# A factor moved as a logarithm into the exponents of the decay matrices, and x copied unscaled by ScalarE

## The reference

```python
alpha = jnp.exp(dt * A)
gamma = lam * dt
beta = (1.0 - lam) * dt * alpha
def step(carry, inp):
    h, prevBx = carry
    x_t, B_t, C_t, a_t, g_t, b_t = inp
    Bx = jnp.einsum('bhp,bhn->bhpn', x_t, B_t)
    h = a_t[..., None, None] * h + g_t[..., None, None] * Bx + b_t[..., None, None] * prevBx
    y = jnp.einsum('bhpn,bhn->bhp', h, C_t)
    return ((h, Bx), y)
y = y + xh * D[None, None, :, None]
y = y * jax.nn.silu(z)
y = _rms(y, norm_w)
return y @ out_proj_w.T
```

## Time and profile before

| | before |
|---|---|
| median of 3 runs | 1303.15 us (1301.98 to 1310.49) |
| profiled execution | 1303.54 us, its span 1301.8 us |
| PE busy | 1149.1 us, 88% |
| DVE busy | 1193.7 us, 92% |
| ACT busy | 811.0 us, 62% |
| POOL busy | 739.4 us, 57% |
| granted TensorE clock, mean | 0.965 |

### The profile page before, as it was taken

The page is one execution under the profiler, slowest core; times in us unless marked ns, Lnnn a source line. Parts: engine busy times, 40 slices in busy tenths (PEclk is TensorE's granted clock), DMA queues, the critical chain, the costliest instruction groups (busy, mean ns, idle before and its releaser), DMA issues. The chain is left out here.

```text
span 1301.8 us, 30976 instructions
## 1 busy us (share of the span) xinstructions
PE 1149.1 (88%) x11530; PEld 837.3 (64%) x11530; DVE 1193.7 (92%) x1925; ACT 811.0 (62%) x1257; POOL 739.4 (57%) x592
## 2 busy tenths in 40 slices
PE   3787489998999999999999899989999899989996
PEld 3662266666666666666666667666667666666664
DVE  7988499998999899998999899989999899989994
ACT  4576166666666666667666666656666666666663
POOL 5000166665766566665766576656666576666664
PEclk9865699999999999999999999999999999999999
DMA  8533343234332153333333343234332333322330
GB/s 189 182 97 105 94 100 69 69 66 99 91 82 64 43 124 83 67 70 73 86 83 71 78 101 73 56 70 116 90 68 59 79 91 83 68 53 59 84 67 9
DMA packets 69664, 107.75 MB, mean 83 GB/s; under 512 B 14179, under 2 KB 32844, under 8 KB 69196
## 3 DMA queue, kind: packets, MB, share of 16 engines
q1 hardware_dynamic: 69516, 105.78, 34.8%
HBM read 24.73 MB, written 12.06 MB: 28 GB/s over the span
## 5 line engine op out<-in xcount | busy, mean ns | idle before, releaser
L1403 POOL TENSOR_TENSOR rot<-part 128x512 f32<-128x512 f32 x256 | 375.8, 1469 | 515.6 <-DVE part L1207 515.6
L1207 DVE SCALAR_TENSOR_TENSOR part<-bcs,k_prmT,k_trig 128x512 f32<-128x512 f32 x512 | 495.9, 1017 | 22.7 <-DMA bcs<-bc_t 12.1
L1340 ACT ACTIVATE E<-d 128x512 f32<-128x512 f32 x256 | 151.7, 592 | 186.4 <-PE d L1029 186.4
L1225 DVE TENSOR_TENSOR M<-s,E 128x512 f32<-128x512 f32 x256 | 163.2, 676 | 2.4 <-PE s L1047 1.8
L1047 PE MATMUL s<-rot 64*128 64x128 f32 x2048 | 149.7, 285 | 17.2 <-POOL rot L1403 17.1
L1047 PEld LDWEIGHTS s<-rot 64*128 64x128 f32 x2048 | 126.9, 188 | 55.1 <-issue 54.7
L1412 POOL TENSOR_TENSOR ce<-rot,eb 128x512 f32<-128x512 f32 x128 | 160.2, 1273 | 3.0 <-ACT eb L1373 3.0
L1456 POOL TENSOR_TENSOR sqa<-sqa,sq 128x512 f32<-128x512 f32 x112 | 142.5, 1273 | 14.5 <-ACT sq L1345 6.2
L1013 PE MATMUL r<-k_w_zx,xns 128*128 128x256 f32 x512 | 133.1, 382 | 12.1 <-DMA xns<-xn_t 12.1
L1136 PE MATMUL y<-M,xk 128*64 128x128 f32 x2048 | 140.1, 279 | 0.0
L1061 PEld LDWEIGHTS o<-k_w_o,yT 128*128 128x128 f32 x1024 | 132.5, 191 | 10.5 <-DVE yT L1298 5.0
(11 more groups left out here) (244 smaller groups left out, 1823.0 us busy)
## 6 DMA issues: line engine op xcount, KB each, us to landing
k_trig<-k_tri SPq DMA_DIRECT2D x512, 128.0 KB, 2.4
bcs<-bc_t SPq DMA_DIRECT2D x16, 256.0 KB, 3.9
bcs<-bc_t SPq DMA_DIRECT2D x32, 128.0 KB, 3.8
a_big<-in_L_attn_u SPq DMA_DIRECT2D x4, 512.0 KB, 6.1
xn_t<-a_xnT SPq DMA_DIRECT2D x1, 2048.0 KB, 14.7
tc_t<-a_tcT SPq DMA_DIRECT2D x1, 2048.0 KB, 16.8
bc_t<-a_tmp SPq DMA_DIRECT2D x1, 2048.0 KB, 7.7
gate_rows<-a_big SPq DMA_DIRECT2D x8, 256.0 KB, 2.0
```

The costliest lines, as they stand in the source:

```text
L1207: nc.vector.scalar_tensor_tensor(out=part[:, 2 * p + f, :], in0=bcs[:, (t + q // NQ) % 2, 2 * w + f, :], scalar=col, in1=trig[:, p, 1 - f, ...
L1225: nc.vector.tensor_tensor(M[:, h, :], Sp[h % 2][:], E[:, h % 2, :], ALU.mult).then_inc(m_ready, 1)
L1340: nc.scalar.activation(E[:, h % 2, :], Dp[:], ACT.Exp).then_inc(e_ready, 1)
L1403: nc.gpsimd.tensor_tensor(rot[:, q % 2, p, w, :], part[:, 2 * p, :], part[:, 2 * p + 1, :], ALU.add).then_inc(rot_ready, 1)
```

## The change

The state's input factor kk leaves x. For the decay matrices its logarithm is cut into three bf16 parts like the running sum and takes 12 more rows of K["pick"] (123 rows instead of 111), so that Exp gives exp(cum[t] - cum[s]) kk[s]. For the state, `dec` is multiplied by kk once in `prepare`. `xk` then holds plain x: ScalarE copies it, and DVE keeps only the product with `cc`, which waits for ScalarE's copy (`x_copied`) instead of PE's product.

```diff
@@ prepare: vector
-                for dst, head in PLACES:
-                    link(nc.vector.tensor_tensor(by4(K["kk"][:, a:b])[:, :, dst], by4(gam[:, a:b])[:, :, head],
-                                                 by4(ps[i][:])[:, :, head], ALU.add))
+                link(nc.vector.tensor_tensor(kk[:, a:b], gam[:, a:b], ps[i][:], ALU.add))
+                nc.vector.tensor_scalar(kk[:, a:b], kk[:, a:b], 0.0, TINY, ALU.max, ALU.add).then_inc(kk_done, 1)
@@ prepare: gpsimd (own_log, the mask of the new rows, is built before)
+            for i in range(2):
+                pool.wait_ge(log_cut, i + 1)
+                nc.gpsimd.tensor_tensor(s[2].rearrange("p (c h) -> p c h", h=H), s[2].rearrange("p (c h) -> p c h", h=H), cum3[:, :, H * i:H * i + H], ALU.subtract).then_inc(log_left, 1)
+            pool.wait_ge(dec_done, 1)
+            nc.gpsimd.tensor_tensor(K["dec"][:], K["dec"][:], kk[:], ALU.mult).then_inc(log_left, 1)
@@ prepare: tensor, in the loop of the gate
+                if t in (3, 4):
+                    pe.wait_ge(log_cut, 3)
+                    for g in (2 * t - 6, 2 * t - 5):
...
+                        for i in range(8):
+                            last = nc.tensor.transpose(ps_bf[g % 2][0:3 * H, i, :], cum3[:, 8 * g + i, :], K["ident_bf"][:])
+                        last.then_inc(logT_t, 1)
@@ prepare: scalar
+                if g == 2:
+                    act.wait_ge(kk_done, 2)
+                    nc.scalar.activation(s[2], kk[:], ACT.Ln).then_inc(log_left, 1)
...
+            def log_part(i):
+                act.wait_ge(log_left, i + 1)
+                act.wait_ge(cumT_t, 4)
+                nc.scalar.copy(cum3[:, :, H * i:H * i + H], s[2].rearrange("p (c h) -> p c h", h=H)).then_inc(log_cut, 1)
+
+            log_part(0)
             for t in range(NS):
                 if t + 2 < NS:
                     gate_input(t + 2)
+                if t in (1, 3):
+                    log_part((t + 1) // 2)
...
+                if t in (3, 4):
+                    act.wait_ge(cum_stored, 64)
+                    for g in (2 * t - 6, 2 * t - 5):
+                        act.wait_ge(logT_t, g + 1)
+                        nc.scalar.copy(cumT[:, 1024 * g:1024 * g + 1024],
+                                       ps_bf[g % 2][0:3 * H].rearrange("p c t -> p (c t)")).then_inc(logT_out, 1)
@@ prepare: sync
-            fill(cum[OWN_S:D_ROWS], own[OWN_S:D_ROWS, :], 8)
+            fill(cum[OWN_S:OWN_L], own[OWN_S:OWN_L, :], 8)
+            fill(cum[OWN_L:D_ROWS], own_log[OWN_L:D_ROWS, :], 8)
...
+                if t == 5:
+                    sp.wait_ge(logT_out, 4)
+                    for i in range(3):
+                        sp.dma_start(logs_d.rearrange("t c i h s -> i h (t c) s")[i],
+                                     cumT[H * i:H * i + H, :].rearrange("h (x s) -> h x s", s=P)).then_inc(logs_stored, 16)
@@ units: sync
+                sp.dma_start(K["pick"][OWN_L:D_ROWS, :], logs_d[t].rearrange("c i h s -> (c i) (h s)")).then_inc(cum_loaded, 16)
@@ units: vector, x_scaled
-                dve.wait_ge(x_ready, at(T2, t, 2 * q + i + 1))
+                dve.wait_ge(x_copied, at(T2, t, 2 * q + i + 1))
                 dve.wait_ge(y_ready, at(T2, t, 2 * q - 2))
-                for dst, f in ((xk, "kk"), (xc, "cc")):
-                    v = K[f][:, tt * (CS * H) + 2 * i * H:tt * (CS * H) + 2 * i * H + 2 * H].rearrange("p (c h) -> p c h", h=H)
...
@@ units: scalar
+            def x_copy(t, q, i):
+                act.wait_ge(x_ready, at(T2, t, 2 * q + i + 1))
+                act.wait_ge(y_ready, at(T2, t, 2 * q - 2))
+                nc.scalar.copy(xk[:, q % 2, 2 * i:2 * i + 2, :].rearrange("p c k -> p (c k)"), R[i][:]).then_inc(x_copied, 1)
...
                     decays(t, q, 2)
                     decays(t, q, 3)
+                    if live(t, q + 1):
+                        x_copy(t, q + 1, 0)
                     for p in range(2):
                         act.wait_ge(eb_ready, at(T2, t, 2 * q + p + 1))
                         act.wait_ge(ce_ready, at(T2, t, 2 * q - 1 + p))
                         nc.scalar.activation(eb[:, p, :], Dp[:], ACT.Exp).then_inc(ebs_ready, 1)
+                    if live(t, q + 1):
+                        x_copy(t, q + 1, 1)
```

More of the change, by code:

```diff
@@ L49 @@
 OWN_S = OWN_T + 3
-D_ROWS = OWN_S + 3 * CS
+OWN_L = OWN_S + 3 * CS
+D_ROWS = OWN_L + 3 * CS
 ODD_T = 123
@@ L299, in _ @@
                 link(nc.gpsimd.tensor_copy(tile[0:MASK_ROWS, 1:CS, :], bcast(tile[0:MASK_ROWS, 0:1, :], [MASK_ROWS, CS - 1, P])))
-            mine = own[OWN_T:D_ROWS, :].rearrange("r (c s) -> r c s", c=CS)
+            mine = own[OWN_T:OWN_L, :].rearrange("r (c s) -> r c s", c=CS)
             link(nc.gpsimd.memset(own[64:P, :], 0.0))
-            link(nc.gpsimd.memset(own[OWN_T:D_ROWS, :], -1.0))
+            link(nc.gpsimd.memset(own[OWN_T:OWN_L, :], -1.0))
             for base, mult in ((-3, 1), (5, -1)):
@@ L307, in _ @@
             link(nc.gpsimd.memset(own[OWN_T:OWN_S, :], 1.0))
+            mine = own_log[OWN_T:D_ROWS, :].rearrange("r (c s) -> r c s", c=CS)
+            link(nc.gpsimd.memset(own_log[OWN_T:D_ROWS, :], 1.0))
+            for base, mult in ((-3 - 3 * CS, 1), (5 + 3 * CS, -1)):
+                link(nc.gpsimd.affine_select(out=mine, in_=mine, compare_op=ALU.is_ge, fill=0.0, base=base,
+                                             pattern=[[-3 * mult, CS], [0, P]], channel_multiplier=mult))
             pool.sem_inc(masks, 1)
@@ L580, in _ @@
             link(nc.vector.scalar_tensor_tensor(out=s[1], in0=s[2], scalar=-1.0, in1=s[1], op0=ALU.add, op1=ALU.subtract))
-            link(nc.vector.scalar_tensor_tensor(out=s[0], in0=s[0], scalar=0.0, in1=K["kk"][:], op0=ALU.max, op1=ALU.add))
+            link(nc.vector.scalar_tensor_tensor(out=s[0], in0=s[0], scalar=0.0, in1=kk[:], op0=ALU.max, op1=ALU.add))
             dve.wait_ge(inv_done, 2)
@@ L809, in _, with units @@
                 nc.scalar.activation(fgate[:, t % 2, :], ps[2 + t % 2][:], ACT.Silu, scale=sc[:, 5:6]).then_inc(g_done, 1)
-def units(nc, K, u, scratch, cum_stored, out):
-    xn_d, tc_d, bc_d, cum_d, cumt_d, gate_d = scratch
+                if t in (3, 4):
[4 more added lines that the diff above has]
+                                       ps_bf[g % 2][0:3 * H].rearrange("p c t -> p (c t)")).then_inc(logT_out, 1)
+def units(nc, K, u, scratch, cum_stored, logs_stored, out):
+    xn_d, tc_d, bc_d, cum_d, cumt_d, gate_d, logs_d = scratch
     with ExitStack() as ctx:
@@ L870, in units @@
         xk_ready, bw_ready = sem("xk_ready"), sem("bw_ready")
+        x_copied = sem("x_copied")
         sz_ready, yt_ready, sq_ready = sem("sz_ready"), sem("yt_ready"), sem("sq_ready")
@@ L954, in _ @@
             sp.wait_ge(cum_stored, 64)
+            sp.wait_ge(logs_stored, 48)
             load_cum(0)
@@ L1318, in _ @@
             act.sem_inc(absd, 3)
-            for s in (e_ready, ebs_ready, sz_ready, sq_ready, acc_done):
+            for s in (e_ready, ebs_ready, x_copied, sz_ready, sq_ready, acc_done):
                 act.sem_inc(s, 1)
@@ L1360, in normalised @@
                 last.then_inc(acc_done, 1)
+            x_copy(0, 0, 0)
+            x_copy(0, 0, 1)
             decays(0, 0, 0)
@@ L1476, in program @@
         cum_stored = ctx.enter_context(nc.semaphore("cum_stored"))
-        prepare(nc, K, dram, scratch, cum_stored)
-        units(nc, K, dram[0], scratch, cum_stored, out)
+        logs_stored = ctx.enter_context(nc.semaphore("logs_stored"))
+        prepare(nc, K, dram, scratch, cum_stored, logs_stored)
+        units(nc, K, dram[0], scratch, cum_stored, logs_stored, out)
 NAMES = ["u", "in_proj_w", "dt_bias", "A_log", "D", "B_norm_w", "C_norm_w", "B_bias", "C_bias", "norm_w", "out_proj_w"]
```

40 lines of the change are left out of this document (25 added, 15 removed).

## The result

| | before | after |
|---|---|---|
| median | 1303.99 us (4 runs, 1301.98 to 1310.49) | 1327.59 us (4 runs, 1326.39 to 1329.10) |
| ratio to before | | 1.0173 (95% interval 1.0135 to 1.0210) |
| profiled execution | 1303.54 us | 1327.3 us, its span 1325.6 us |

The account below looks back on a forecast made before the run. It took the loop to be bound by a chain through PE's stretch from bw to x half 1 and DVE's half 1. Terms 15.8 + 6.4 + 0.5 - 0.6 = 22.1 on 1303.5 gave 1325 us, range 1308 to 1340.

Parts of the forecast that it names:

- The loop's chain: Per unit: bw, PE's stretch to x half 1, DVE's half 1, M2, M3, six rotations, two yT, bw; half 0 outside.
- Copy for product in half 1: In the chain, ScalarE's copy replaces DVE's product of 0.60 us, leaving the link as long: +0.01 to +0.03 us.
- The copy ahead of eb: ScalarE's half 0 copy makes the first eb 0.25 us later, delaying PE's second row exponents and x half 1 by 0.24.
- 63 x 0.25: The loop's loss: 63 units with a next unit, each 0.25 us longer, 15.8 us in all.
- Other consequences hide: In the loop, z, the table load and Silu, the 12 more rows and the extra transfer cost nothing.
- GpSimd in `prepare`: GpSimd's three 1024-column instructions beside DVE's `quantise` cost DVE 6.4 us, between nothing and 7.6.
- One more fill: SP issues one more fill ahead of the stores before the loop: +0.5 us (0 to 1).
- ScalarE's extra work hidden: In `prepare`, ScalarE's Ln, table load, casts and copies find gaps and cost nothing; uncovered, 1 to 2 us.
- Rival A: DVE itself is the loop, so two products fewer save 1.20 us per unit: 1234 us; chance 0.09 with its half way.
- A's half way: GpSimd collides less with DVE in the moved order, each freed sum giving back 1.06 us per unit; within the 0.09.
- B: No change to speak of: the copy ahead of eb is absorbed, 1305 to 1312 us; chance 0.14.
- C: Slower still: longer copies and added waits cost 0.45 us per unit, 1340 us; chance 0.07.

Follow-up runs that it names:

- e2: The kernel before without DVE's product into xk of half 0, which stays zero: 1301.94 us, ratio 0.9988.
- e3: The kernel before without DVE's product into xk of half 1, which stays zero: 1288.37 us, ratio 0.9878.
- e12: The kernel of e3, also without GpSimd's second ce of each unit but the first: 1265.01 us, ratio 0.9699.
- e4: The changed kernel with ScalarE's copies of halves 0 and 1 behind the first and second eb: 1318.05 us, repeated at 1310.17 us.
- e1: The kernel before plus one unread ScalarE copy per unit ahead of the first eb: 1320.42 us, ratio 1.0129.
- e8: The changed kernel without GpSimd's three instructions in `prepare`: 1323.50 us, ratio 1.0136.
- e9: The changed kernel with xc directly behind PE's x, ScalarE's copies behind both eb and xc, and its root ahead of them: 1310.91 us, ratio 1.0033.

## Why the prediction held, step by step

- **The loop's chain** (bw, PE's stretch, DVE's half 1, M, rotations, yT): right, but for q = 2 of every second super-chunk, where DVE came to half 1 without a wait for PE. e2 shows that half 0 isn't in it, e3 and e12 that half 1 is, with 0.59 us (predicted 0.60).
- **Copy for product in half 1**: right. e4's middle unit has both copies and no delay of eb, and takes 17.22: +0.03.
- **The copy ahead of eb**: right in mechanism and size. eb is 0.28 later (predicted 0.25), PE 0.27, the period 0.30. PE's second row exponents wait for eb in 55 places, where it was 8. e1 alone and e4 alone show it from both sides.
- **63 x 0.25**: the sum is right with two errors in it. Middle units lost 0.29 to 0.30, those with q = 1 only 0.12, and q = 2 of every second super-chunk 0.17, so the mean was 0.26. In q = 1 PE has one product more (o from k_cum and k_zeros_bf) ahead of its second row exponents, which started at 6.47 after bw and not at 6.30 even before the change. They start at 6.57 now, so the first 0.17 of the delay was free. That 63 x 0.25 came so close to 16.3 is in part luck. I had read one middle unit, and a q = 0 unit for the wait only.
- **DVE's idle time before xc** of 1.6 us: 1.68. Its share of about 84%: 85%.
- **Other consequences hide**: right for the loop (e1 has none of them, and its units lose 15.7 of the change's 16.3 us). The product with 123 rows takes 390 ns as the one with 111 did.
- **GpSimd in `prepare`**, 6.4 (0 to 7.6): 5.8, by three collisions and not by six halves; even the instruction with one input was caught (0.43 became 2.46). The Trainium skill ("SBUF — State Buffer", Who interferes with whom) has it that whoever issues first keeps the shared ports for its whole instruction. The rows agree: each DVE instruction ends one own length or less after GpSimd's. The sum of 7.6 was too high mainly because an instruction on 1024 columns takes less than twice 1.27: the second subtraction, which meets nothing, takes 2.12 us, so three are 6.4, and DVE lost 5.8 of them.
- **One more fill**, +0.5: wrong sign in the trace. The first `quantise` of the loop came at 101.97 where it was 104.27 before, 2.3 earlier. Upstream of it ScalarE had waited 6.79 us for the store of tc_t to land, and now waits 3.45. Why it landed earlier stays open.
- **ScalarE's extra work hidden**: wrong in part. Not predicted were PE's wait of 1.69 us for the cast (L495), after which DVE stood 0.78 and 1.18 us for PE, and a last Silu that started 1.2 later behind DVE's last `quantise` than before: the 3.1 us that e8 still has. Nor did I see that the second stage's first transfer would stand 5.01 us behind the last Silu's start, where it had been 3.34: 1.7 more. I had put this whole term at nothing.
- **The first unit**: -0.8 (predicted -0.6).
- **The sum up to the first bw**: 5.8 + 3.1 + 1.7 - 2.3 - 0.8 = 7.5, against 6.4 + 0.5 - 0.6 = 6.3. That these are so close is luck: 4.8 us that I had not seen were half covered by an earlier start that I had not seen either.
- **Rival A** falls with e2: removing work from the engine with the highest share gave 0.1%, within its interval of no change. The Trainium skill ("Perfetto Trace Analysis", Identifying the Most-Contended Engine) would have begun there. A's half way, fewer collisions in the moved order, did not come about: the six rotations still take 6.10 (only in q = 2 of every second super-chunk did 6.20 become 6.10). **B** falls: no part of the delay was absorbed in the middle units, and 0.17 of it in those with q = 1. **C**'s 0.45 per unit did not occur.

## What to carry to other kernels

Before work is moved to a less busy engine, look at what stands behind the new instruction in that engine's order, and whom it serves: one copy of 0.58 us ahead of an exponential, on an engine with over a third of its time free, cost 16 us, and behind it nothing. Count a saving only up to where the next engine stands idle, and in each kind of unit, not in one. When a chain gets shorter, ask what its instructions will now run beside: GpSimd's ce, which used to end as DVE's rotations began, took back 0.43 of 0.59 us.

## What the hardware showed that I had not expected

- VectorE beside GpSimd: six rotations take 6.09 to 6.10 us when they begin after ce, 6.52 when they begin 0.6 us before its end, 7.18 when they begin 1.9 before. This is no gradual slowing. In the trace of before every rotation of over 1 us, 173 of them, ends 0.55 to 0.56 us after a GpSimd instruction; met by none, it takes 0.74. In `prepare` too DVE's instruction waits out GpSimd's whole remaining length.
- TensorE's clock: in e9 the same gap of 1.90 us on PE stands in all seven units with a root. In five it was followed by 1.2 GHz for about 3 us, and a unit of 20.39 us took 21.6; in two the clock stayed at 2.4 GHz. What decides between them stays open. In the first stage one and the same `prepare` took 160 or 167 us, with the granted clock at 1.00 or at 0.59 to 0.73 between 30 and 50 us. Two single profiles of such kernels can't be compared by their ends, only stretch by stretch.
